# Gated delta-rule attention with an eight-expert FFN: the order of VectorE's small operations and one slot of TensorE's order changed

## The reference

```
x = L0_attn_x
x = _layernorm(x + _L0_attn_ref(x, ...), axis=-1)
x = _layernorm(x + _L0_ffn_ref(x, ...), axis=-1)
```

```
q = _short_conv(x @ Wq, conv_q)            # 4 taps over time, then SiLU; k and v alike, 3 each per head
g = -jnp.exp(A_log) * jax.nn.softplus(x @ Wa + dt_bias)
def step(S, inp):
    S = S * jnp.exp(gt)[..., None, None]
    for i in range(nh):
        kS = jnp.einsum('bhd,bhde->bhe', ki, S)
        S = S + bi[..., None, None] * (ki[..., None] * (vi - kS)[:, :, None, :])
    o = jnp.einsum('bhd,bhde->bhe', qt, S)
    return (S, o)
...
o = o * jax.lax.rsqrt(jnp.mean(o * o, -1, keepdims=True) + 1e-05) * rms_weight
o = o * jax.nn.silu(gate)
return o.reshape(b, t, h * dv) @ Wo
```

## Time and profile before

| | us |
|---|---|
| median of 3 runs | 8508.51 |
| lowest and highest | 8502.43, 8517.87 |
| the profiled execution's own time | 8499.04 |
| its span from first to last instruction | 8497.0 |
| mean granted TensorE clock | 0.956 |
| PE busy in the span | 7561.9 (89%) |
| DVE busy in the span | 6595.7 (78%) |
| ACT busy, POOL busy | 5290.1 (62%), 4106.0 (48%) |

### The profile page before, as it was taken

The page is one execution under the profiler, slowest core; times in us unless marked ns, Lnnn a source line. Parts: engine busy times, 40 slices in busy tenths (PEclk is TensorE's granted clock), DMA queues, the critical chain, the costliest instruction groups (busy, mean ns, idle before and its releaser), DMA issues. The chain is left out here.

```text
span 8497.0 us, 425999 instructions
## 1 busy us (share of the span) xinstructions
PE 7561.9 (89%) x155940; PEld 6383.7 (75%) x155940; DVE 6595.7 (78%) x22297; ACT 5290.1 (62%) x19575; POOL 4106.0 (48%) x6333
## 2 busy tenths in 40 slices
PE   5788988888889888888888889889898889979999
PEld 1677777777777777777777777777777777857777
DVE  3888888888888888888888888888888888733333
ACT  2566666666666666666666666666666666623333
POOL 0355555555555555555555555555555555511111
PEclk6799999999999999999999999999999999989999
DMA  2000000000000000000000000000000000010000
GB/s 86 5 9 9 9 10 9 9 9 9 10 9 10 9 9 9 9 10 9 10 10 9 10 9 9 10 8 10 9 9 9 10 9 10 8 29 10 7 10 8
DMA packets 283622, 97.66 MB, mean 11 GB/s; under 512 B 226096, under 2 KB 276544, under 8 KB 281152
## 3 DMA queue, kind: packets, MB, share of 16 engines
q1 hardware_dynamic: 281408, 68.93, 3.7%
HBM read 52.08 MB, written 16.78 MB: 8 GB/s over the span
## 5 line engine op out<-in xcount | busy, mean ns | idle before, releaser
L802 DVE SCALAR_TENSOR_TENSOR CY<-PP,CWV,CY 128x128 f32<-128x128 f32 x4608 | 1590.3, 345 | 102.2 <-ACT CY L721 1.4
L802 DVE SCALAR_TENSOR_TENSOR CY<-PP,CWK,CY 128x128 f32<-128x128 f32 x4608 | 1587.4, 344 | 83.9
L1004 POOL TENSOR_TENSOR UM<-U,C 32x256 f32<-32x256 f32 x1536 | 1104.8, 719 | 120.2 <-POOL UM L1004 20.8
L997 POOL TENSOR_TENSOR Y<-U,C 32x256 f32<-32x256 f32 x768 | 553.9, 721 | 1201.0 <-DVE UQ L880 1160.9
L516 PE MATMUL PP<-XT,WK 128*128 128x131 f32 x3072 | 741.5, 327 | 262.0 <-DVE CY L802 251.5
L516 PE MATMUL PP<-XT,WV 128*128 128x131 f32 x3072 | 756.6, 333 | 239.8 <-DVE CY L802 212.3
L977 POOL TENSOR_TENSOR S<-R,BETA 96x4 f32<-96x4 f32 x512 | 101.4, 198 | 1606.6 <-DVE R L840 1606.6
L536 PE MATMUL PI<-T,WB 32*32 32x32 f32 x49152 | 732.6, 194 | 138.7 <-DVE T L811 133.7
L536 PEld LDWEIGHTS PI<-T,WB 32*32 32x32 f32 x49152 | 623.2, 109 | 298.6 <-issue 230.2
L721 ACT ACTIVATE CY<-PP,CWK 128x128 f32<-128x128 f32 x1536 | 560.7, 365 | 453.8 <-PE PP L516 447.4
L820 DVE SCALAR_TENSOR_TENSOR S<-S,WHOLE,PK 128x128 f32<-128x128 f32 x2048 | 612.6, 341 | 253.1 <-PE PK L591 252.9
(11 more groups left out here) (228 smaller groups left out, 19080.8 us busy)
## 6 DMA issues: line engine op xcount, KB each, us to landing
EX<-exd SPq DMA_DIRECT2D x768, 32.0 KB, 2.2
exd<-EXS SPq DMA_DIRECT2D x16, 512.0 KB, 2.6
XR<-in_L_attn_x SPq DMA_DIRECT2D x65, 64.0 KB, 2.7
XL<-in_L_attn_x SPq DMA_DIRECT2D x16, 256.0 KB, 2.8
XRES<-in_L_attn_x SPq DMA_DIRECT2D x64, 64.0 KB, 3.0
x<-X SPq DMA_DIRECT2D x64, 64.0 KB, 1.6
XI<-x SPq DMA_DIRECT2D x16, 256.0 KB, 2.8
out<-OUT SPq DMA_DIRECT2D x16, 256.0 KB, 2.3
```

Of the source, the lines that this page charges most:

```text
L802: dve.scalar_tensor_tensor(CY[:, m % RING], ptile(m)[:, s:s + P], taps_of(m)[:, s:s + 1], CY[:, m % RING], ALU.mult, ALU.add).then_inc(tap ...
L997: pool.tensor_tensor(Y1[r, :, :], U[r, par, :, r], over(first[r, :], [BK, NHEAD, BK], 1), ALU.mult).then_inc(seed_sb, 1)
L1004: pool.tensor_tensor(UM[r, lv], U[r, par, :, r], over(merge[lv][r, :], [BK, NHEAD, BK], 1), ALU.mult).then_inc(made, 1)
```

## The change

Seven things are placed differently. No arithmetic is changed, and no instruction is added or removed.

1. On PE, `new_state` moves from slots 11 and 12 to slots 10 and 11, for each half of the heads.
2. On DVE, the inverse's writes move from the border of the slot into part 0, behind tap 1. The two kinds of transposes behind them move to part 1, behind tap 2.
3. On DVE, `add_state` for heads 4 to 7 moves from two pairs in slot 0 to four single instructions in slots 0 and 1.
4. On DVE, the reciprocal `R` moves from part 0 to part 1, behind tap 2.
5. `QSE` moves from part 0 to part 1.
6. `YL` moves from slot 12, part 0 of chunk 2, to slot 13, part 1. The statistics follow in slots 0 and 1 of chunk 3, one in each part, and `X1` moves from slot 1 to slot 4 of chunk 3.
7. On POOL, `RS` moves from the end of chunk 2's program to chunk 3's, behind the diagonal copy `YF`.

```diff
-                        if k in (11, 12) and do_run:
-                            new_state(k - 11, run, rc, prep, do_prep)
+                        if k in (10, 11) and do_run:
+                            new_state(k - 10, run, rc, prep, do_prep)
...
-                def add_state(l, run, part):
+                def add_state(l, run, part, parts):
                     if part == 0:
                         dve.wait_ge(s_ps, 2 * run + l + 1)
-                    for h in heads[l][2 * part:2 * part + 2]:
+                    for h in heads[l][LH // parts * part:LH // parts * (part + 1)]:
...
-                    if k == 0 and known(run - 1, 0, NCH):
-                        add_state(1, run - 1, part)
+                    if do_inv and k in INV_AT and INV_AT[k] not in (0, 4) and part == 0:
+                        inv_out(invn, INV_AT[k])
+                    if do_inv and INV_AT.get(k) == 3 and part == 1:
+                        dve.wait_ge(inv_sb, STEPS * invn + 4)
+                        flip(XB, Y2).then_inc(x2t_sb, 1)
+                    if do_inv and INV_AT.get(k) == 7 and part == 1:
+                        dve.wait_ge(inv_sb, STEPS * invn + 8)
+                        need(dve, join_ps, 3 * (invn - 1) + 1)
+                        for b in range(2):
+                            r = slice(BK * b, BK * b + BK)
+                            op = dve.transpose(X3[r, :, r], Y3[r, :, :])
+                        op.then_inc(x3t_sb, 1)
+                    if k in (0, 1) and known(run - 1, 0, NCH):
+                        add_state(1, run - 1, 2 * k + part, 4)
...
+                    if k in (3, 5) and do_prep and part == 1:
+                        l = k // 5
                         dve.wait_ge(sse_sb, 2 * prep + l + 1)
                         need(dve, kds_sb, 2 * prep - 1 + l)
                         dve.reciprocal(R2[0:R, lanes[l]], SSE[0:R, lanes[l]]).then_inc(r2_sb, 1)
-                    if k == 10 and c == 3 and do_prep and part == 0:
+                    if k == 10 and c == 3 and do_prep and part == 1:
...
-                        add_state(0, run, part)
-                    if k == 12 and out_now and part == 0:
+                        add_state(0, run, part, 2)
+                    if k == 13 and out_now and part == 1:
                         q = i - 2
                         dve.wait_ge(wo_ps, q + 1)
...
                         dve.tensor_tensor(YL[:, :], PB[:, 0:P], XRES[:, half], ALU.add).then_inc(y_sb, 1)
-                        dve.wait_ge(y_sb, q + 1)
+                    if k == 0 and norm_now and part == 0:
+                        dve.wait_ge(y_sb, i - 1)
                         dve.bn_stats(ST[:, :], YL[:, :]).then_inc(st_sb, 1)
-                        dve.wait_ge(st_sb, q + 1)
+                    if k == 0 and norm_now and part == 1:
+                        dve.wait_ge(st_sb, i - 1)
                         dve.memset(spare[:, :], 0.0)
                         dve.bn_aggr(MV[:, :], ST[:, :]).then_inc(mv_sb, 1)
-                        dve.wait_ge(mv_sb, 2 * q + 1)
+                    if k == 1 and norm_now and part == 0:
+                        dve.wait_ge(mv_sb, 2 * (i - 2) + 1)
                         dve.tensor_scalar(MV[:, 1:2], MV[:, 1:2], EPS_LN, None, ALU.add).then_inc(mv_sb, 1)
-                    if k == 1 and c == 3 and known(i - 2, 0, NSC) and part == 0:
+                    if k == 4 and norm_now and part == 1:
...
+                    if c == 3 and known(i - 2, 0, NSC):
+                        pool.wait_ge(mv_sb, 2 * (i - 1))
+                        need(pool, x1_sb, i - 2)
+                        pool.tensor_tensor(RS[:, :], MV[:, 1:2], mhalf[:, 0:1], ALU.pow).then_inc(rs_sb, 1)
```

More of the change, by code:

```diff
@@ L814, in flip @@
                     return dve.transpose(to[:, :, :].rearrange("p h c -> p (h c)"), of[:, :, :].rearrange("p h c -> p (h c)"))
-                def add_state(l, run, part):
+                def add_state(l, run, part, parts):
                     if part == 0:
                         dve.wait_ge(s_ps, 2 * run + l + 1)
-                    for h in heads[l][2 * part:2 * part + 2]:
+                    for h in heads[l][LH // parts * part:LH // parts * (part + 1)]:
                         op = dve.scalar_tensor_tensor(S[:, h], S[:, h], WHOLE[:, run, h:h + 1], PK[:, h], ALU.mult, ALU.add)
-                    if part == 1:
+                    if part == parts - 1:
                         op.then_inc(s_sb, 1)
@@ L826, in group @@
                     ahead, prep, invn, run, do_ahead, do_prep, do_inv, do_run = when(i, c)
+                    norm_now = c == 3 and known(i - 2, 0, NSC)
                     rc, par = (c - 2) % 4, c % 2
@@ L911, in program @@
                     for k in range(SLOTS):
-                        if do_inv and k in INV_AT and INV_AT[k] not in (0, 4):
-                            inv_out(invn, INV_AT[k])
-                            if INV_AT[k] == 3:
-                                dve.wait_ge(inv_sb, STEPS * invn + 4)
-                                flip(XB, Y2).then_inc(x2t_sb, 1)
-                            if INV_AT[k] == 7:
-                                dve.wait_ge(inv_sb, STEPS * invn + 8)
-                                need(dve, join_ps, 3 * (invn - 1) + 1)
-                                for b in range(2):
-                                    r = slice(BK * b, BK * b + BK)
-                                    op = dve.transpose(X3[r, :, r], Y3[r, :, :])
-                                op.then_inc(x3t_sb, 1)
                         j, jh, m = lagged(i, half, SLOTS * c + k - 1)
@@ L1005, in program @@
                                 pool.wait_ge(made, NBK * prep + b + 1)
-                    if c == 2 and known(i - 2, 0, NSC):
-                        pool.wait_ge(mv_sb, 2 * (i - 1))
-                        need(pool, x1_sb, i - 2)
-                        pool.tensor_tensor(RS[:, :], MV[:, 1:2], mhalf[:, 0:1], ALU.pow).then_inc(rs_sb, 1)
                 pool.wait_ge(ready, READY)
```

## The result

| | before | after |
|---|---|---|
| median of 4 runs, us | 8505.47 | 8392.32 |
| lowest and highest, us | 8498.15, 8517.87 | 8364.65, 8422.8 |
| profiled execution: time, span, us | 8499.04, 8497.0 | 8395.38, 8393.3 |
| mean granted TensorE clock in it | 0.956 | 0.938 |

The ratio is 0.9865, with a 95% interval of 0.9838 to 0.9892. The kernel became 113 us faster. The forecast was 273 us of gain, and the gain is less than half of that. The time lies inside the stated 8150 to 8400 only because that range was stretched to take in two rivals; it is 88 us above the 8304 that the forecast's own working allows. The last row of the table is the first hint at the reason: the new kernel ran at a lower mean clock than the old one.

A forecast was written before the change was run, and what follows sets the result against it. A ring of PE's run (slot 4 to new state) and DVE's (state sum to slot 3) bounds each chunk. Gains of 4.4 us over 62 steps, 273 us, take 8508.5 to about 8230; range 8168 to 8304, stretched to 8150 to 8400.

The forecast's parts named there:

- 8304: High bound: PE's wait at 4038.30 stays and gaps of dependent pairs save half, 3.3 us a step, 205 us.
- The sum of 4.4 us a step: Gains over the four chunks of a step, 0.7 + 0.7 + 1.7 + 1.3 us, 273 us over 62 steps.
- `Y3` to `T`, into chunks 3, 0, 1, 2: DVE's run to slot 3: filled tap borders and shorter `Y3` gap save 0.6 us; into chunk 3, added work cancels it.
- `T` to `Y3`, in chunks 0 and 1: State-sum wait goes, but stage 6 of the inversion comes later; 0.1 us remains in each chunk.
- `T` to `Y3`, in chunk 2: `YL` no longer stands ahead of `Y3` (1.26 us), and DVE reaches slot 6's last tap about 0.5 us sooner; 1.7 us.
- `T` to `Y3`, in chunk 3: New state comes ahead of slot 11's projection, the state-sum wait goes, and `Y3` comes 0.7 us sooner.
- Outside that ring waits cost nothing: Only PE's run from slot 4 to new state and DVE's from state sum to slot 3 set a chunk's time.
- PE waiting for `T` above 1 us a chunk: Sign that would show the forecast wrong; PE's wait for the inverse's write `T` was 0.5 us a chunk before.
- The rival "the interleaving saves nothing": Other instructions between DVE's taps save nothing; 2.0 us a step stay, 8385 us; chance 0.08.
- The rival of the late inverse writes: Six inverse writes a chunk each come one tap (0.26 us) later and delay PE's stages; 8634 us; chance 0.05.
- The two rivals with half the gain: Interleaving saves nothing, 8385 us (chance 0.08); or removed waits return at slots 12 and 13, 8415 us (chance 0.09).
- The lower bound: Each step gains 1 us more through PE's waits for taps: 5.5 x 62 = 341 us, so 8168 us.

The follow-up runs named there:

- fill_c2: The changed kernel with PE repeating the four transposes of slot 3 three more times in chunk 2; 8214.63 us, ratio 0.9668 to the kernel before.
- gap_before: The kernel before with two unread 128x512 DVE multiplies ahead of the write `T` in slot 3 of chunk 2; 8798.91 us, ratio 1.0338.
- fa_late: The changed kernel with `FA` of chunk 2 moved behind the write `T`, to slot 3 part 1; 8231.29 us, ratio 0.9692 to the kernel before.
- dve_only: The changed kernel with PE's `new_state` back in slots 11 and 12; 8486.71 us, ratio 0.9981 to the kernel before.
- t_border: The changed kernel with the write `T` of slot 3 back at the border, ahead of tap 1, in all chunks; 8226.6 us, ratio 0.9668 to before.
- fa_t: The changed kernel with `FA` behind `T` and `T` of slot 3 back at the border; 8086.23 us, ratio 0.9496 to the kernel before.
- t_fill: The changed kernel with `T` of slot 3 at the border and slot 3's four transposes repeated three times in chunk 2; 8105.93 us, ratio 0.9525 to before.

## Why the prediction came out as it did

- **The sum of 4.4 us a step** was right, at equal clock: 109.3 to 104.9 us. That it came out to the tenth is partly luck. The table takes the steps at full clock, 11 before and 4 after, from DVE's write `Y3` to its write `T` of slot 3, and from there to the next `Y3`:

  | gained, us | forecast | measured |
  |---|---|---|
  | `Y3` to `T`, into chunks 3, 0, 1, 2 | 0, 0.6, 0.6, 0.6 | 0.18, 0.58, 0.60, -0.01 |
  | `T` to `Y3`, in chunks 0 and 1 | 0.1, 0.1 | 0.41, 0.33 |
  | `T` to `Y3`, in chunk 2 | 1.7 | 1.42 |
  | `T` to `Y3`, in chunk 3 | 0.7 | 0.88 |
  | sum | 4.4 | 4.39 |

  The part into chunk 2 is missing, the one in chunk 2 is too large, and the others, put too small, make up for both. The mechanism of the 0.60 holds where `FA` does not stand. The transposes start 0.60 us behind `Y3` with a tap in between, and the tap itself 0.34 us behind it, which was put at 0.33. `S` and `YL` wait no more, and the waits at `T` and `Y` took part of their place (114.4 us for the 32.3 of `T` before).
- **The step that failed** is one that the prediction never wrote down: it took each matmul at the duration of the kernel before, that is at an unchanged granted clock. It had the column for it in the view that it opened with, 0.97 in the earlier trace rows. The change lowered the mean clock to 0.938, with 11.9 us a step at 1.2 GHz for 6.7, and 160 of the 273 us went that way. `fill_c2` shows it by adding work, `gap_before` by adding a wait.
- **A term was missing on DVE too.** Into chunk 2 the run from `Y3` to `T` kept its 8.17 us (8.19), because the wait for ACT at `FA` grew from 0.24 to 0.70 us. The prediction counted `FA` nowhere, though it stands on the ring. At full clock that is small (0.3 us a step, by `fa_late`), but it falls just where PE waits longest.
- **"Outside that ring waits cost nothing"** was wrong in one respect. PE's waits for taps in slots 0 to 3 cost no time, but they shared PE's idle time out over several places. With faster taps (228.2 to 71.1 us) the idle time was collected at one place, at `T` of chunk 2, from 1.17 to some 2.2 us.
- **PE waiting for `T` above 1 us a chunk** was given as what would prove the forecast wrong, and it came: 1.17 us.
- **The rival "the interleaving saves nothing" is refuted.** The run from `Y3` to `T` is 0.6 us shorter into chunks 0 and 1. `dve_only` saves 2.7 us a step at full clock, though that holds the move of `YL` too. The rows have `X3` 0.60 us behind `Y3` with a whole tap in between, where it was 0.54 with none, so the tap in between cost 0.06 us. The Trainium skill's "VectorE: DVE Perf Modes", section "The DRAIN you can't avoid", says that semaphores between operations cost nothing extra, but also that a next operation which is not held starts earlier. The rows agree with the second sentence, which the prediction passed over: a tap of 0.34 us gives way after 0.26.
- **The rival of the late inverse writes** had the place right. Only one of the six writes was tested, `T` of slot 3, and `t_border` prices its delay at 1.2 us a step at full clock and 166 us in all. The rival asked for 1.1 us passed on in each chunk to turn the sign; what was passed on was 0.3 us, and the clock did the rest. The sign held because the sum behind it was large.
- **The two rivals with half the gain** (8385 and 8415) bracket the measured 8392, but for reasons that were not there. The interleaving saves time, and chunks 0 and 1 did gain at full clock. That their number is close is luck.
- **The lower bound** of 8168 was worked out from 5.5 us a step. The sum and the 1 us more are 5.4, or 8174. It changes nothing here.
- **The others:** `YL` starts 109.5 us apart for a forecast of 107. `Y3` of chunk 2 waits 1.8 us at full clock for a forecast of about 1, and DVE waits at `T` 0.57 us a chunk for some 0.5. PE's share is 0.915 for 0.93. `XB` delayed nothing ahead of stage 4 in the timelines read. `R`, `RS` and `X1` cost nothing that shows.

What stays open: a wait of 2.15 us was followed by full clock in one step and one of 2.28 us by 1.2 GHz in the next. The table above says how often the clock falls behind a wait of a given length at this place. What decides in a single step was not tested. Nor was it tested why nearly every second step has some low clock in every version, `fa_t` too. The traces do show where it sits. Two steps are one pass of the hardware loop, and at each of the 30 borders between passes looked at, in every version, PE stands for 1.9 to 3.6 us ahead of the first projection of chunk 0, as for 3.3 us at 3457.17 in the kernel after. During it or within 6 us of its end a stretch at 1.2 GHz begins in 23 to 30 of the 30 cases (27 before the change, 30 after). With one exception, in `t_fill`, the steps at full clock throughout are those without the border. So this loss is older than the change, and no run here tried to remove it.

## What to carry to other kernels

When an engine beside PE is made faster, ask not only how much PE waits afterwards but in how many pieces: in a kernel whose PE is 90% busy, one wait of 2.2 us in place of two of 1.2 us came with a low clock in the 10 us behind it, and that cost more than half of a real gain. Compare steps at the same granted clock first; it tells at once whether the schedule or the clock is at fault. Then bring forward the write that ends the longest wait, and only if that can't be done, put harmless matmuls in it.

## What the runs showed of the hardware

- In the kernel after, a wait of PE of 2.28 us was followed by 11 us at a granted clock of 0.50, in which PE does 153 matmul records in place of 232 and DVE 26 instructions in place of 38.
- A wait made 1.2 us longer at one place of a step (2.4 for 1.2) cost 285 us in 62 steps, 4.6 us each, about four times its own length.
- Behind one wait of PE at one place of the step, a stretch at 1.2 GHz began in 0 of 56 steps where the wait was up to 1.0 us, in 19 where it was 1.2 to 1.4, in 42 where it was 2.1 to 2.3.
- Twelve repeated 128x128 transposes a step made a kernel 178 us faster, and did nothing (0.9998) in one whose wait was short.
- At each border between two passes of the hardware loop PE stood for 1.9 to 3.6 us, in all 13 versions, and in 23 to 30 of 30 cases a stretch at 1.2 GHz began during it or within 6 us of its end.
